# Gate and up projections of a dense FFN as three float32r products of high and low parts, with the weights split on VectorE

## The chip, the cores and the metric

The kernel runs on one core of a Trainium2 chip. The metric is the device time of one execution in microseconds, as the median of several runs. All times below are microseconds unless marked ns. The engines are TensorE (PE, its weight loads PEld), VectorE (DVE), ScalarE (ACT), GpSimd (POOL) and SyncE (SP), which issues most transfers.

## The reference, cut to what matters

Two layers run one after the other on x, 4 batches of 256 tokens with 256 features. Each layer adds a gated attention and a gated FFN: a retention-like attention and a mixture of 8 experts in layer 0, a grouped-query causal attention with 32 heads of 8 features and a dense FFN in layer 1. The change concerns the last of the four, the dense FFN, and the attention ahead of it only in time.

```python
x = x + jnp.tanh(g_xattn[1]) * _L1_xattn_ref(_layernorm(x), ctx_2048, ctx_2048, ...)
x = x + jnp.tanh(g_ffn[1]) * _L1_ffn_ref(_layernorm(x), w_gate, w_up, w_down)

def _L1_ffn_ref(x, w_gate, w_up, w_down):          # x (4,256,256), w_gate, w_up (256,1024), w_down (1024,256)
    h = jax.nn.silu(jnp.einsum('bsh,hi->bsi', x, w_gate)) * jnp.einsum('bsh,hi->bsi', x, w_up)
    h_sparse = _sparsify_2to4(h)                    # of each 4 neighbours keep the 2 largest in magnitude
    return jnp.einsum('bsi,ih->bsh', h_sparse, w_down)
```

## The kernel before, in words

It is written instruction by instruction: every engine has its own program, in the order of the code, and waits on named semaphores. Tokens are 8 tiles of 128; two halves ("units") of 512 tokens make the moving operand of gate and up. Eight PSUM banks are handed out by `acquire(pe, stage, i, kind)`: a kind is a small ring of banks, and whoever takes a bank waits until the stage that held it is `_taken`. The helper `taken` marks the instruction that reads a bank last. Kind "wide" is banks 0 to 5, "turn1" is bank 6 alone, "tok1" bank 7 alone.

*The last batch of the second attention* (b = 3) is a loop over 24 steps n. In each, TensorE makes a block of scores (`weights`), ScalarE its exponential, GpSimd masks it (`affine_select`), and at odd n one of twelve steps of `finish(2, ...)` ends the batch before: four pairs of transposes in "turn1" (VectorE divides each by its sum: reciprocal and product into `att`), a turn of `att`, the output projection, then on VectorE the residual and the statistics of the next layer norm. At steps 13, 15, 17 and 19 the first four tiles of the layer norm for the FFN go through: VectorE normalizes into `xn` (`norm`), TensorE transposes it (`ln_turn(3, k)`, bank "tok1"), ScalarE copies it to `xT` and thereby frees the bank. At the end come the products with the values.

*The dense FFN* runs over 16 pieces i = 4g + j. A piece is a gate matmul pair and an up matmul pair (`half_piece`, stages "fg" and "fu", contraction over 2 x 128 features, 128 output features x 512 tokens, all f32). ScalarE takes silu of gate, VectorE multiplies by up into `hs`, ScalarE takes the magnitude (`absh`). After each group g of four pieces VectorE runs `sparsify(g, step)` in four steps that stand between the products of the next group: three compares into bf16 (`cmps`, step 0), seven small bf16 sums (`wins`, step 1), and four masking products in steps 2 and 3. The first six pieces also carry the twelve steps of `finish(3, ...)`, and at pieces 3, 4, 6 and 7 TensorE transposes the last four tiles of the layer norm, in "turn1". `down` then multiplies by the third weight, eight tiles of eight f32 matmuls each: the first four wait until the first half of `hs` is masked, the others for the second, and they use two banks in turn, so the third waits for the residual of the first. The residuals of the first four stand between the steps of the last `sparsify` on VectorE.

The gate and up weights lie in the place of the expert weights (`e_gu`), where SyncE loads them as soon as the experts are done, long ahead of the FFN.

## Time and profile before

| | us |
|---|---|
| median of 3 runs | 383.87 |
| lowest and highest run | 381.69, 384.3 |
| span of the profiled execution, first to last instruction | 380.5 |
| of this, the dense FFN from its first matmul to the end | 93.3 |
| granted TensorE clock, mean over the span | 0.946 |

The profile gives the span of the one profiled execution, not a time of its own beside the span; the runs were timed apart. Busy times of the engines overlap, so they say who may be the bound only stretch by stretch. An f32 matmul appears in the trace as two records. The start of the next record on TensorE tells its pace better than a record's own duration, since matmuls are pipelined and their ends are modelled.

### The profile page before, as it was taken

The numbers are of one execution on the slowest core, as the hardware profiler recorded it, in microseconds if no ns is written. First come the engines' busy times: TensorE is split into PE (matmuls) and PEld (weight loads), VectorE is DVE, ScalarE is ACT, GpSimd is POOL, SyncE is SP. The second block draws the span as 40 slices with busy tenths as digits, with TensorE's granted clock in tenths as the row PEclk, the third lists the DMA queues.
The fourth block names the chain that finished last, engine by engine and source line by source line (L and its number), as shares of the span: only waits on it lengthen the run. The fifth ranks groups of instructions, "written<-read, shape, count | busy, mean of one in ns | idle before, by whom it ended". The sixth has DMA issues, their size and how long they took to land.

```text
span 380.5 us, 4562 instructions
## 1 busy us (share of the span) xinstructions
PE 334.3 (88%) x1473; PEld 201.6 (53%) x1473; DVE 220.0 (58%) x513; ACT 156.8 (41%) x327; POOL 100.2 (26%) x154
## 2 busy tenths in 40 slices
PE   3999785969999816999989999998899989999997
PEld 1485574756666404564544654643544444445885
DVE  4345976502222347889956993993342449778911
ACT  2434341333333122136867665774874233333000
POOL 7203663520000176401342334333441001000000
PEclk9999998588999756799999999999999999999999
DMA  7997000153111114500000000000000000000011
GB/s 231 364 421 210 0 15 2 65 167 101 46 53 41 55 56 166 221 0 9 0 8 2 0 0 9 0 3 8 0 2 0 2 0 0 0 1 2 28 41 41
DMA packets 14023, 22.53 MB, mean 59 GB/s; under 512 B 2049, under 2 KB 11393, under 8 KB 13186
## 3 DMA queue, kind: packets, MB, share of 16 engines
q1 hardware_dynamic: 13234, 20.16, 15.3%
q0 software_dynamic: 768, 2.10, 1.7%
q8 instruction: 12, 0.20, 0.2%
q14 instruction: 9, 0.07, 0.1%
HBM read 15.96 MB, written 6.03 MB: 58 GB/s over the span
## 4 chain that ended last, share of the span: by engine, by line
PE 65%; DVE 14%; issue 6%; POOL 5%; ACT 5%; DMA 4%; SPq 1%; ACTq 0%; DVEq 0%; POOLq 0%
PE bank L241 47%; DVE mx L1216 6%; PE bank L458 5%; PE bank L426 4%; ACT region L929 3%; PE bank L429 3%; POOL x_sorted L739 2%; PE bank L257 2%; DVE stats L999 2%; PE bank L251 2%; POOL rstd L711 1%; DVE x_sb L1039 1%; PE bank L473 1%; DMA x_sb<-in_x_dram 1%; PE bank L510 1%
## 5 line engine op out<-in xcount | busy, mean ns | idle before, releaser
L929 ACT ACTIVATE region<-bank,padcol 128x512 f32<-128x512 f32 x96 | 62.4, 695 | 18.1 <-PE bank L241 17.3
L1216 DVE TENSOR_REDUCE mx<-bank 128x2 f32<-128x512 f32 (+1 forms) x96 | 61.3, 683 | 11.7 <-PE bank L429 11.4
L241 PE MATMUL bank<-xT,e_gu 128*128 128x512 f32 x128 | 57.6, 594 | 0.5 <-ACT xT L792 0.5
L775 POOL TENSOR_SCALAR_AFFINE_SELECT region<-region 128x1024 f32<-128x1024 f32 x32 | 35.0, 1094 | 81.8 <-ACT region L929 81.7
L241 PE MATMUL bank<-qst,kblk 128*128 128x512 f32 x96 | 46.1, 490 | 0.8 <-DMA qst<-nmT 0.3
L426 PE MATMUL bank<-kblk,qst 128*128 128x512 f32 x96 | 45.1, 488 | 1.7 <-ACT qst L877 0.9
L241 PEld LDWEIGHTS bank<-xT,e_gu 128*128 128x128 f32 x128 | 23.3, 190 | 25.1 <-issue 24.3
L429 PE MATMUL bank<-causb,identb 128*128 128x256 bf16 (+1 forms) x96 | 31.8, 331 | 0.0
L241 PE MATMUL bank<-e_down,region 128*128 128x256 f32 x128 | 27.8, 379 | 0.0
L707 POOL TENSOR_SCALAR veps<-mv 128x1 f32<-128x1 f32 x40 | 11.4, 284 | 62.0 <-DVE mv L1001 59.9
L241 PEld LDWEIGHTS bank<-e_down,region 128*128 128x128 f32 x128 | 24.3, 190 | 3.7 <-issue 0.5
L1039 DVE SCALAR_TENSOR_TENSOR x_sb<-bank,tg,x_sb 128x256 f32<-128x256 f32 x24 | 11.6, 483 | 24.9 <-PE bank L241 24.8
L792 ACT ACTIVATE xT<-bank 128x256 f32<-128x256 f32 x32 | 12.3, 385 | 32.0 <-PE bank L251 31.9
L711 POOL TENSOR_TENSOR rstd<-veps,power 128x1 f32<-128x1 f32 x40 | 23.8, 595 | 3.3
L251 PE MATMUL bank<-ident,xn 128*128 128x128 f32 x48 | 12.2, 350 | 13.9 <-DVE xn L1011 11.2
L458 PE MATMUL bank<-region,vaug 128*32 128x512 f32 x192 | 23.9, 600 | 0.2
L241 PEld LDWEIGHTS bank<-qst,kblk 128*128 128x128 f32 x96 | 18.6, 196 | 9.6 <-ACT region L929 7.1
L426 PEld LDWEIGHTS bank<-kblk,qst 128*128 128x128 f32 x96 | 19.2, 200 | 8.3 <-issue 4.5
L984 ACT ACTIVATE silu<-bank 128x512 f32<-128x512 f32 x16 | 9.6, 597 | 32.5 <-PE bank L241 32.5
L1188 DVE TENSOR_TENSOR sact<-bank,silu 128x176 f32<-128x176 f32 x15 | 5.1, 342 | 30.8 <-ACT silu L895 30.8
L241 PE MATMUL bank<-e_gu,sT 128*128 x60 | 21.8, 489 | 0.5 <-ACT sT L889 0.5
L241 PE MATMUL bank<-e_down,sT 128*128 (+1 forms) x60 | 19.6, 426 | 1.4 <-ACT sT L910 1.4
(158 smaller groups left out, 543.9 us busy)
## 6 DMA issues: line engine op xcount, KB each, us to landing
e_gu<-in_e_gu_dram SPq DMA_DIRECT2D x2, 1408.0 KB, 11.9
x_sorted<-zero SPq DMA_DIRECT2D x1, 1920.0 KB, 9.1
y_sorted<-region SPq DMA_DIRECT2D x15, 128.0 KB, 1.7
x_sb<-in_x_dram SPq DMA_DIRECT2D x4, 256.0 KB, 4.2
ctxT<-in_ctxT_dram SPq DMA_DIRECT2D x2, 512.0 KB, 6.1
e_down<-in_e_down_dram SPq DMA_DIRECT2D x1, 1024.0 KB, 13.7
region<-x_sorted SPq DMA_DIRECT2D x1, 1024.0 KB, 7.3
e_gu<-in_f_gate_dram SPq DMA_DIRECT2D x1, 1024.0 KB, 4.8
```

The lines of the kernel that those rows point to most:

```text
L241: return pe.matmul(dst, lhsT, rhs, start=first, stop=last)
L251: ins = pe.transpose(dst[:, tile_cols(t)], src[:, tile_cols(t)], ident[:, :])
L426: pe.matmul(dst, qst[:, s, q, hg, tile_cols(nt)], kblk[s][q][:, quads, 0:(nt + 1) * P], start=True, stop=False, skip_group_check=True)
L429: ready(pe.matmul(diagonal, identb[:, :], causb[:, 0:diagonal.shape[1], :], start=False, stop=True, skip_group_check=True), "sa")
L458: ins = pe.matmul(dst[32 * j:32 * j + 32, :], vaug[:, 2 * b + mt, 4 * q + j, :], rhs, start=(mt == 0), stop=(mt == nt), skip_group_check=True)
L707: pool.tensor_scalar(veps[:, layer, k:k + 1], mv[:, layer, k, 1:2], eps, None, ALU.add)\
L711: pool.tensor_tensor(out=rstd[:, layer, k:k + 1], in0=veps[:, layer, k:k + 1], in1=power[:, :], op=ALU.pow).then_inc(sem(f"rstd{layer}"), 1)
L775: pool.affine_select(out=block, in_=block, compare_op=ALU.is_ge, fill=0.0, base=0, pattern=[[0, 2], [0, PER_GROUP], [1, P]], channel_multi ...
L792: taken(act.activation(xT[:, :, tile_cols(tile)], src[:, 0:DIM].rearrange("p (t n) -> p t n", t=KT), ACT.Copy), f"ln{layer}")
L929: taken(act.activation(dst, src.rearrange("p (h n) -> p h n", n=SEQ - mt * P), ACT.Exp, bias=padcol[:, key:key + 1], scale=float(HD) ** -0 ...
L1039: dve.scalar_tensor_tensor(out=x_sb[:, tile, :], in0=filled(dve, stage, k)[:, 0:DIM], scalar=tg[:, g:g + 1], in1=x_sb[:, tile, :], op0=ALU ...
L1216: taken(dve.reduce_max(mx[:, b % 2, nt, quads, q, hg], src, AX), "sa")
```

## The change

Gate and up no longer multiply f32 by f32. The transposed x and both weights are kept as a float32r high part and a float32r remainder, and each product is the sum of three: high x high, low x high and high x low. The product of the two low parts is left out. A piece of gate or up is thus six float32r matmuls instead of two f32 ones.

The high part of x is what ScalarE's copy writes (`x_high`, in the place of `xT`); a new step on VectorE, `norm_low`, subtracts it from the bank (`x_low`, in the place of `qhi` and `qlo`) and is now what frees the bank. Early tiles do this one step after the transposes (n - 1 in NORM_STEPS), late ones at pieces 4, 5 and 7 (LATE_LOW). The weights are split by eight VectorE instructions, `split_weights`, at eight steps of the last attention batch (SPLIT_AT): a cast into the high part, a subtraction in place for the low part. `gate_high` takes the place of `ctxT`, the halves of `up_high` the rest of `e_gu` and `sT`; the compares (`cmps`) move from `ctxT` to `qst`. The transposes of the last tile move from behind the up matmuls of piece 7 to before them. Several semaphores are merged, so that one count stands for several start-up loads or constants.

```diff
+LATE_LOW = {4: (4,), 5: (5,), 7: (6, 7)}
+SPLIT_AT = (0, 2, 4, 5, 6, 8, 9, 10)
...
-        cmps = ctxT[:, :, :].rearrange("p t n -> p (t n)").bitcast(BF16).rearrange("p (c n) -> p c n", n=UNIT)
+        gate_low = sb_over("gate_low", [P, KT, FFN_I], F32R, "e_gu")
+        up_low = sb_over("up_low", [P, KT, FFN_I], F32R, "e_gu", 4 * KT * FFN_I)
+        gate_high = sb_over("gate_high", [P, KT, FFN_I], F32R, "ctxT")
+        up_high = (sb_over("up_high0", [P, FFN_I], F32R, "e_gu", 8 * KT * FFN_I), sb_over("up_high1", [P, FFN_I], F32R, "sT"))
+        x_high = sb_over("x_high", [P, KT, TOKENS], F32R, "xT")
+        x_low = sb_over("x_low", [P, KT, TOKENS], F32R, "qhi")
+        halves = {"fg": ([gate_high[:, t, :] for t in range(KT)], gate_low, f_gate),
+                  "fu": ([up_high[t][:, :] for t in range(KT)], up_low, f_up)}
+
+        cmps = sb_over("cmps", [P, 6, UNIT], BF16, "qst")
...
-            def half_piece(stage, w, g, j):
+            def half_piece(stage, g, j):
+
                 u, blk = divmod(g, FFN_BLOCKS)
                 us = slice(u * UNIT, (u + 1) * UNIT)
-                c = j * 2 * P + blk * P
+                c = slice(j * 2 * P + blk * P, j * 2 * P + blk * P + P)
+                high, low, _ = halves[stage]
                 dst = acquire(pe, stage, 4 * g + j, "wide")
                 for t in range(KT):
-                    ins = mm(dst, w[:, t, c:c + P], xT[:, t, us], t == 0, t == KT - 1)
+                    mm(dst, high[t][:, c], x_high[:, t, us], t == 0, False)
+                    mm(dst, high[t][:, c], x_low[:, t, us], False, False)
+                    ins = mm(dst, low[:, t, c], x_high[:, t, us], False, t == KT - 1)
                 ready(ins, stage)
...
             pe.wait_ge(sem("ln3_taken"), UNIT_TILES)
+            pe.wait_ge(sem("w_split"), 4 * KT)
             loaded(pe, "f", 3)
             for n in range(8):
-                half_piece("fg", f_gate, n // 4, n % 4)
+                half_piece("fg", n // 4, n % 4)
                 if 2 * n < 12:
                     finish(BATCH - 1, 2 * n)
-                half_piece("fu", f_up, n // 4, n % 4)
+                if n == 7:
+                    ln_turn(3, TILES - 1, "turn1")
+                half_piece("fu", n // 4, n % 4)
                 if 2 * n < 12:
                     finish(BATCH - 1, 2 * n + 1)
-                if n in LATE_NORM_STEPS:
+                if n in LATE_NORM_STEPS[:3]:
                     ln_turn(3, UNIT_TILES + LATE_NORM_STEPS.index(n), "turn1")
...
-                taken(act.activation(xT[:, :, tile_cols(tile)], src[:, 0:DIM].rearrange("p (t n) -> p t n", t=KT), ACT.Copy),
-                      f"ln{layer}")
+                if layer == 3:
+                    act.activation(x_high[:, :, tile_cols(tile)], src, ACT.Copy).then_inc(sem("x_high_made"), 1)
+                else:
+                    taken(act.activation(xT[:, :, tile_cols(tile)], src, ACT.Copy), f"ln{layer}")
...
+            def norm_low(k):
+
+                src = filled(dve, "ln3", k)[:, 0:DIM].rearrange("p (t n) -> p t n", t=KT)
+                dve.wait_ge(sem("x_high_made"), k + 1)
+                taken(dve.tensor_tensor(out=x_low[:, :, tile_cols(k)], in0=src, in1=x_high[:, :, tile_cols(k)].bitcast(F32),
+                                        op=ALU.subtract), "ln3")
+
+            def split_weights(i):
+
+                stage, t = (("fg", 0), ("fg", 1), ("fu", 0), ("fu", 1))[i // 2]
+                high, low, raw = halves[stage]
+                if i == 0:
+                    loaded(dve, "f", 3)
+                if i % 2 == 0:
+                    dve.tensor_copy(high[t], raw[:, t, :]).then_inc(sem("w_split"), 1)
+                else:
+                    dve.wait_ge(sem("w_split"), i)
+                    dve.tensor_tensor(out=low[:, t, :], in0=raw[:, t, :], in1=high[t].bitcast(F32), op=ALU.subtract)\
+                       .then_inc(sem("w_split"), 1)
...
+                    if b == BATCH - 1 and n - 1 in NORM_STEPS:
+                        norm_low(NORM_STEPS.index(n - 1))
                     if b == BATCH - 1 and n + 2 in NORM_STEPS:
                         norm(3, NORM_STEPS.index(n + 2))
+                    if b == BATCH - 1 and n in SPLIT_AT:
+                        split_weights(SPLIT_AT.index(n))
...
+                    for k in LATE_LOW.get(i, ()):
+                        norm_low(k)
                     if 2 * i < 12:
                         finish(BATCH - 1, 2 * i)
                     src = filled(dve, "fu", i)
```

The order of instructions at three places follows. In brackets stands what an instruction waits for.

On VectorE, early in the last attention batch (`rden` and `att` are the division of `finish(2, ...)`, `x_sb` its residual), before:

```order
L1001 BN_AGGR mv<-stats 128x2 [waits stats]
L1249 RECIPROCAL rden<-bank 128x8 [waits avT_ready,atT_ready]
L1251 TENSOR_TENSOR att<-bank,rden 128x8x8 [waits rden_made]
L1249 RECIPROCAL rden<-bank 128x8 [waits avT_ready]
L1251 TENSOR_TENSOR att<-bank,rden 128x8x8 [waits rden_made]
...
L1039 SCALAR_TENSOR_TENSOR x_sb<-bank,tg,x_sb 128x256 [waits res2_ready,bias_added]
```

and after, the first of the four pairs of divisions and the stretch ahead of the residual:

```order
L1270 CAST gate_high<-e_gu 128x1024 [waits in_f]
L1293 RECIPROCAL rden<-bank 128x8 [waits avT_ready,atT_ready]
L1295 TENSOR_TENSOR att<-bank,rden 128x8x8 [waits rden_made]
L1273 TENSOR_TENSOR gate_low<-e_gu,gate_high 128x1024 [waits w_split]
...
L1295 TENSOR_TENSOR att<-bank,rden 128x8x8 [waits rden_made]
L1273 TENSOR_TENSOR up_low<-e_gu,up_high_52 128x1024 [waits w_split]
L1270 CAST up_high_53<-e_gu 128x1024
L1273 TENSOR_TENSOR up_low<-e_gu,up_high_53 128x1024 [waits w_split]
L1064 SCALAR_TENSOR_TENSOR x_sb<-bank,tg,x_sb 128x256 [waits res2_ready,bias_added]
```

Eight instructions now stand between the divisions and ahead of the residual.

On VectorE, at the change from the first group of four pieces to the second (`region` is `hs`), before:

```order
L1357 TENSOR_TENSOR region<-bank,silu 128x512 [waits fg_taken,fu_ready]
L1249 RECIPROCAL rden<-bank 128x8 [waits avT_ready]
L1251 TENSOR_TENSOR att<-bank,rden 128x8x8 [waits rden_made]
L1316 TENSOR_TENSOR ctxT<-region 128x1536 [waits abs_made]
L1318 TENSOR_TENSOR ctxT<-region 128x1024
L1320 TENSOR_TENSOR ctxT<-region 128x512
L1357 TENSOR_TENSOR region<-bank,silu 128x512 [waits fg_taken,fu_ready]
```

and after:

```order
L1407 TENSOR_TENSOR region<-bank,silu 128x512 [waits fg_taken,fu_ready]
L1293 RECIPROCAL rden<-bank 128x8 [waits avT_ready]
L1295 TENSOR_TENSOR att<-bank,rden 128x8x8 [waits rden_made]
L1364 TENSOR_TENSOR cmps<-region 128x1536 [waits abs_made]
L1366 TENSOR_TENSOR cmps<-region 128x1024
L1368 TENSOR_TENSOR cmps<-region 128x512
L1260 TENSOR_TENSOR x_low<-bank,x_high 128x2x128 [waits x_high_made,ln3_ready]
L1407 TENSOR_TENSOR region<-bank,silu 128x512 [waits fg_taken,fu_ready]
```

The subtraction for the sixth tile (`x_low`, which frees the bank "turn1") stands behind the three compares.

On TensorE, around piece 5, before (`xn` is the sixth tile of the layer norm, `att` the turn of `finish(3, 10)`):

```order
L251 MATMUL bank<-ident,xn 128x128
L241 MATMUL bank<-xT,e_gu 128x512 [waits fg_taken]
L241 MATMUL bank<-xT,e_gu 128x512
L257 MATMUL bank<-ident,att 128x128 [waits ln3_taken,avT_taken]
L257 MATMUL bank<-ident,att 128x128
L241 MATMUL bank<-xT,e_gu 128x512 [waits fu_taken]
```

and after:

```order
L269 MATMUL bank<-ident,xn 128x128
L259 MATMUL bank<-x_high,gate_high 128x512 [waits fg_taken]
L259 MATMUL bank<-x_low,gate_high 128x512
L259 MATMUL bank<-x_high,gate_low 128x512
...
L275 MATMUL bank<-ident,att 128x128 [waits ln3_taken,avT_taken]
L275 MATMUL bank<-ident,att 128x128
L259 MATMUL bank<-x_high,up_high_52 128x512 [waits fu_taken]
```

The transposes wait for the same count `ln3_taken` as before; what raises it has moved from ScalarE's copy to VectorE's subtraction.

## Rows read from the trace of the kernel before

**Rows 1.** Busy time by stretch: us, PE, PEld, DVE, ACT, POOL, PEclk, DMA share, GB/s.

```profile
287.20:322.50 35.30, 32.95 (x104) 16.14 (x100) 19.16 (x47) 11.89 (x23) 2.04 (x4) 1.00 0.00 0
322.50:350.10 27.60, 27.59 (x65) 12.29 (x66) 21.53 (x36) 9.39 (x17) 0.00 (x0) 1.00 0.00 1
```

**Rows 2.** Timeline of PE in the FFN: start, duration, engine, instruction, idle before.

```profile
287.17 1.98 PE L241 MATMUL bank<-xT,e_gu 128*128 128x512 f32 x4
...
309.77 0.44 PE L251 MATMUL bank<-ident,xn 128*128 128x128 f32 x2 [0.94 <-DVE att L1251]
...
325.61 24.63 PE L241 MATMUL bank<-xT,e_gu 128*128 128x512 f32 x57
350.08 27.79 PE L241 MATMUL bank<-e_down,region 128*128 128x256 f32 x128
```

**Rows 3.** Timeline of PE: float32r matmuls of the attention, at full clock.

```profile
198.70 0.29 PE L241 MATMUL bank<-qhi,selr 128*128 128x256 f32 x1
198.82 0.28 PE L241 MATMUL bank<-qlo,selr 128*128 128x256 f32 x1
...
205.09 0.40 PE L426 MATMUL bank<-kblk,qst 128*128 128x512 f32 x1
205.33 0.28 PE L429 MATMUL bank<-causb,identb 128*128 128x256 bf16 x1
```

**Rows 4.** Timeline of ACT behind the second late transposes.

```profile
310.24 0.38 ACT L792 ACTIVATE xT<-bank 128x256 f32<-128x256 f32 x1 [2.93 <-PE bank L251]
310.52 0.62 ACT L978 ACTIVATE region<-region 128x512 f32<-128x512 f32 x1
```

**Rows 5.** Timeline of DVE in the FFN.

```profile
315.19 0.47 DVE L1039 SCALAR_TENSOR_TENSOR x_sb<-bank,tg,x_sb 128x256 f32<-128x256 f32 x1
...
316.57 0.68 DVE L1325 TENSOR_TENSOR amat<-ctxT 128x1024 bf16<-128x1024 bf16 x1
...
326.24 0.69 DVE L1357 TENSOR_TENSOR region<-bank,silu 128x512 f32<-128x512 f32 x1 [2.50 <-PE bank L241]
326.85 1.75 DVE L1316 TENSOR_TENSOR ctxT<-region 128x1536 bf16<-128x1536 f32 x1
...
330.25 0.68 DVE L1357 TENSOR_TENSOR region<-bank,silu 128x512 f32<-128x512 f32 x1
...
333.59 0.68 DVE L1357 TENSOR_TENSOR region<-bank,silu 128x512 f32<-128x512 f32 x1
334.19 1.28 DVE L1346 SCALAR_TENSOR_TENSOR region<-amat,region 128x512 f32<-128x512 bf16 x2
```

**Rows 6.** Timeline of DVE in the last attention batch.

```profile
266.07 0.21 DVE L1249 RECIPROCAL rden<-bank 128x8 f32<-128x8 f32 x1 [2.71 <-PE bank L473]
...
273.16 0.48 DVE L1039 SCALAR_TENSOR_TENSOR x_sb<-bank,tg,x_sb 128x256 f32<-128x256 f32 x1 [3.25 <-PE bank L241]
...
276.31 0.41 DVE L1011 TENSOR_SCALAR xn<-x_sb,mv,rstd 128x256 f32<-128x256 f32 x1
...
277.39 0.69 DVE L1011 TENSOR_SCALAR xn<-x_sb,mv,rstd 128x256 f32<-128x256 f32 x1
```

**Rows 7.** Timeline of POOL in the last attention batch: causal masks.

```profile
268.13 1.10 POOL L775 TENSOR_SCALAR_AFFINE_SELECT region<-region 128x1024 f32<-128x1024 f32 x1 [3.33 <-ACT region L929]
...
276.84 1.09 POOL L775 TENSOR_SCALAR_AFFINE_SELECT region<-region 128x1024 f32<-128x1024 f32 x1 [2.73 <-ACT region L929]
```

**Rows 8.** Groups of DVE by shape, whole span: busy us, mean ns.

```profile
L1034 DVE TENSOR_SCALAR amat<-amat 128x256 f32<-128x256 f32 x2 | 0.6, 294 | 0.1
L1318 DVE TENSOR_TENSOR ctxT<-region 128x1024 bf16<-128x1024 f32 x4 | 4.9, 1220 | 0.0
```

**Rows 9.** Busy time by stretch, as rows 1: an idle stretch and two of low clock.

```profile
80.50:83.50 3.00, 0.00 (x1) 0.01 (x1) 0.04 (x1) 0.34 (x2) 0.00 (x0) 1.00 0.44 129
84.80:88.10 3.30, 3.30 (x7) 2.01 (x8) 0.28 (x1) 1.78 (x3) 0.00 (x0) 0.50 0.99 325
149.50:156.20 6.70, 5.97 (x19) 3.85 (x19) 5.08 (x12) 1.68 (x4) 5.41 (x11) 0.50 0.96 406
```

More of the change, by code:

```diff
@@ L51, in build_program, with sb_over @@
     with ctx:
+        homes = {}
         def sb(name, shape, dt=F32):
+            homes[name] = (nc.sbuf_base + 31) // 32 * 32
             return ctx.enter_context(nc.sbuf_tensor(name, shape, dt))
+        def sb_over(name, shape, dt, home, skip=0):
+            return nc.alloc_sbuf_tensor_at(name, shape, dt, offset=homes[home] + skip)
         sems = {}
@@ L329, in _ @@
             gate(1)
-            loaded(pe, "wo0")
-            loaded(pe, "router")
+            loaded(pe, "wo0", 2)
             for k in range(TILES + 4):
@@ L344, in _ @@
                     logits(k - 4)
-            pe.wait_ge(sem("onehot_made"), 1)
-            loaded(pe, "tri")
+            pe.wait_ge(sem("routed"), 1)
+            loaded(pe, "caus", 3)
             dst = acquire(pe, "rank", 0, "main")[:, 0:(TILES + 1) * EXPERTS].rearrange("p (k e) -> p k e", e=EXPERTS)
@@ L406, in keys @@
                     pe.wait_ge(sem("sel_made"), 2)
-                    pe.wait_ge(sem("padrow_made"), 1)
+                    pe.wait_ge(sem("pads_made"), 1)
                 pe.wait_ge(sem("kp_taken"), b + 1)
@@ L641, in _ @@
             load(sp, "gates", gates[:, 2:4], a["g_f"])
-            load(sp, "decay", decay[:, :, :], a["decay"])
+            load(sp, "gates", decay[:, :, :], a["decay"])
             load(sp, "wg", wg[:, :, :], a["wg"])
@@ L646, in _ @@
             load(sp, "wo0", wo0[:, :, :], a["wo0"])
-            load(sp, "router", router[:, :, :], a["router"])
-            load(sp, "small", small_c[:, :], a["small"])
+            load(sp, "wo0", router[:, :, :], a["router"])
+            load(sp, "sel", small_c[:, :], a["small"])
             load(sp, "sel", sel_in, a["sel"])
@@ L653, in _ @@
             load(sp, "sel", mask_col[:, :], a["mask_col"])
-            load(sp, "tri", tri[:, :, :], a["tri"])
-            sp.wait_ge(sem("zero_set"), 1)
+            load(sp, "caus", tri[:, :, :], a["tri"])
+            sp.wait_ge(sem("constants_set"), 1)
             sp.dma_start(x_sorted.rearrange("(s p) n -> p s n", p=P),
@@ L696, in _ @@
         def _(pool):
-            pool.memset(zero[:, :], 0.0).then_inc(sem("zero_set"), 1)
-            pool.memset(power[:, :], -0.5).then_inc(sem("power_set"), 1)
-            pool.memset(vaug[:, :, :, :], 1.0).then_inc(sem("ones_set"), 1)
-            pool.memset(amat[:, :, :], 1.0).then_inc(sem("a_set"), 1)
-            pool.wait_ge(sem("power_set"), 1)
+            pool.memset(zero[:, :], 0.0).then_inc(sem("constants_set"), 1)
+            pool.memset(power[:, :], -0.5).then_inc(sem("constants_set"), 1)
+            pool.memset(vaug[:, :, :, :], 1.0).then_inc(sem("constants_set"), 1)
+            pool.memset(amat[:, :, :], 1.0).then_inc(sem("constants_set"), 1)
+            pool.wait_ge(sem("constants_set"), 2)
             chain = [0]
@@ L734, in _ @@
             pool.wait_ge(sem("blocks_clear"), HALVES)
-            pool.wait_ge(sem("placed"), 1)
+            pool.wait_ge(sem("routed"), 3)
             pool.wait_ge(sem("sorted_zeroed"), 16)
@@ L829, in _ @@
                     ln_turn(1, k - 3)
-            act.wait_ge(sem("vdiff"), 1)
+            act.wait_ge(sem("routed"), 2)
             act.activation(r_s[:, 3, :], r_s[:, 2, :], ACT.Exp).then_inc(sem("vexp"), 1)
@@ L840, in projections @@
                 if b == 0:
-                    act.wait_ge(sem("ones_set"), 1)
+                    act.wait_ge(sem("constants_set"), 3)
                 for t in range(2):
@@ L895, in slot_silu @@
                 act.activation(silu[:, i % 2, 0:EXPERT_I], src, ACT.Silu).then_inc(sem("silu_made"), 1)
-            act.wait_ge(sem("padrow_made"), 1)
+            act.wait_ge(sem("pads_made"), 1)
             slot_turn(0)
@@ L922, in exponentials @@
                 if n == 0 and b == 0:
-                    act.wait_ge(sem("padcol_made"), 1)
+                    act.wait_ge(sem("pads_made"), 2)
                     act.wait_ge(sem("x2"), TILES)
@@ L1020, in _ @@
                     norm(0, k - 2)
-            loaded(dve, "decay")
-            dve.wait_ge(sem("a_set"), 1)
+            loaded(dve, "gates", 3)
+            dve.wait_ge(sem("constants_set"), 4)
             for h in range(RET_HEADS):
@@ L1041, in residual @@
                    .then_inc(sem(stage + "_taken"), 1)
-            loaded(dve, "sel", 3)
-            loaded(dve, "small")
+            loaded(dve, "sel", 4)
             dve.tensor_scalar(padrow[:, :], mask_row, 0.0, MASKED, ALU.is_equal, ALU.mult)\
-               .then_inc(sem("padrow_made"), 1)
+               .then_inc(sem("pads_made"), 1)
             dve.tensor_scalar(padcol[:, :], mask_col[:, :], 0.0, DEAD, ALU.is_equal, ALU.mult)\
-               .then_inc(sem("padcol_made"), 1)
+               .then_inc(sem("pads_made"), 1)
             def gn_center(k):
```

24 lines of the change are left out of this document (12 added, 12 removed).

## The prediction

> **What bounds the kernel now.** I read the last 93 us of the span, because the change leaves everything up to the fourth batch of the second attention as it was. First the table of busy time by stretch [rows 1]: while gate and up run, TensorE is busy 32.95 of 35.30 us and then 27.59 of 27.60, and VectorE 19.16 and 21.53. So TensorE is the bound there, but VectorE has only about 6 us in hand in the second stretch. Then TensorE's timeline [rows 2]: the dense FFN begins at 287.17, the first of 32 pieces of gate or up (two f32 matmuls, four records) takes some 1.8 us, and late in the stretch 57 records take 24.47 us, 0.43 us each or 1.72 us a piece. The down projection then runs 128 records of 0.217 us without a gap and ends the kernel. The granted clock is 1.00 throughout. VectorE's steady round for four pieces is in [rows 5]: product 0.61, compares 3.40 (326.85 to 330.25), product 0.61, counts 2.73, then twice a product and a pair of masking products, 0.60 and 1.28. That is 11.1 us, against 8 x 1.72 = 13.8 us of TensorE.
>
> **TensorE's pieces.** A piece becomes six float32r matmuls of 512 columns. The nearest rows [rows 3]: two float32r matmuls of 256 columns, each with its own stationary load, start 0.12 us apart; one of 512 columns is followed after 0.24 us. Between twice 0.1067 (256 columns at 2.4 GHz) plus 0.003 (the overhead of a 0.43 us f32 record) and 0.24 I take 0.225, nearest to the first row's overhead of 0.011: 1.35 us a piece, bounds 1.30 and 1.44. All 32 pieces then save 32 x 0.37 = 11.8 us of TensorE. The Trainium skill, "TensorE: Matmul & The Clock Gate", section "Back-to-back issue gap", gives columns over 2.4 GHz plus about 2.5 ns; an estimate from it is 0.216 us, and the sum below would be better by 0.7 us. The row of 0.12 us at full clock shows more overhead than that.
>
> **VectorE's subtractions hold a bank.** This is where most of the saving goes. Before, ScalarE's copy released the bank of each normalized tile; now VectorE's subtraction x_low releases it, and the four late ones use the one bank that TensorE's attention transposes need as well. The order of VectorE puts x_low of the sixth tile behind the 3.40 us of compares, and TensorE's next transposes wait for it. Before, from 287.17 to the second late transposes at 309.77 [rows 2] is 22.60 us: ten pieces (17.2) and 5.4 of transposes and waits, which stay. With 1.35 a piece they come 18.9 us after the start. ScalarE copies the tile and then takes the magnitudes that the compares need: these end 1.37 after the transposes [rows 4]; compares 3.40, and x_low with its hand-over 0.48 (as the residual at 315.19 [rows 5], the same 256 columns). So TensorE goes on 5.29 us after the transposes; with 0.27 for them and 1.35 for one piece it **stands 3.67 us**.
>
> Then it needs 0.22 for the waiting transposes, 1.35 for a piece, and 1.13 for the attention's last projection (four records of 0.217) and the hand-over; VectorE spends 1.40 on residual, statistics and normalization (315.19 to 316.57 and a hand-over [rows 5]), 2.73 on counts, 0.60 and 0.32 on product and normalization, 1.28 on masking, and 0.48 on x_low of the seventh tile. Only then may the last tile be transposed, 33.7 us after the start, while TensorE has finished everything ahead of that after 30.95: it **stands 2.76 us** more. Three pieces and 0.47 of transposes and hand-over later the ninth product runs, at 38.2 us. Before it ran at 326.24, 39.07 after the start. **In the first half the FFN gains 0.8 us**, not 6.
>
> From the ninth product on TensorE (8 x 1.35 = 10.8 a round) is ahead of VectorE (11.1), and VectorE's rounds set the time: 11.1 to the thirteenth product, then 9.2 to the sixteenth, 20.3; before, the sixteenth ran 0.2 after 350.08, 24.0 later: **3.7 gained**. At the end the down projection's third tile waits for the first one's residual, which now comes behind the last product, masking, compares and residual: 5.86; six tiles of 16 x 0.217 follow, 20.7, so 26.6 from the sixteenth product to the end, and before 27.4: **0.8 gained**. In all 5.3 us, with VectorE as the bound and not TensorE.
>
> **The split in the last attention phase.** Eight instructions of 1,024 columns. A subtraction is priced by the f32 compare of that size, 1.22 busy [rows 8] and, as products of 0.69 follow one another after 0.61 [rows 5], about 1.14 to the next start; a cast has no row: at one column a cycle 1.22, at the rate of the f32 operation with one input in [rows 8] (256 columns in 0.294 where a residual takes 0.48) about 0.69 and 0.60 to the next. I take the latter, the row nearest in kind. VectorE is idle 2.71 us before 266.07 [rows 6], so the first cast is free; the other seven and the three pairs between them fill it from 266.07 to 273.9, and the residual that stood at 273.16 comes 0.75 later. On it hang the normalization, the transposes and, in turn, all that follows. GpSimd's causal masks of 1.1 us run in the same stretch [rows 7], and where one runs, a VectorE operation with one input waits: the normalization at 277.39 took 0.69 instead of the usual 0.41, ending when the mask that began at 276.84 was over. I count one such wait, 0.5. The four early x_low release their bank 0.45 after the copy did, and this shifts the start of the last values once: 0.45. Sum 1.7 us; bounds 0.5 (the queue of exponentials absorbs the rest) and 3.9 (casts at one column a cycle, +1.6, and one more half mask, +0.6). Loads of the weights are long done, ScalarE's eight copies cost what they did, cmps only moves, and the merged semaphores of the start wait for loads that were waited for anyway: nothing.
>
> **The clock.** After the idle stretch 80.5 to 83.5 the granted clock fell to 0.50 (1.2 GHz) some 1.3 us after work had begun again, for 3.3 us; another low stretch lasted 6.7 us [rows 9]. The waits of 0.94 us at 309.77 left it at full. Both new stands are well over the latter, so I expect a fall after each, as in the first of these rows. After the first, 1.3 us cover the waiting piece and the projection behind it takes 0.86 more; the next two pieces are not waited for. After the second, two pieces that are waited for run in the low stretch: half of 3.3, 1.65. Together 2.5; bounds 0 and, low from the start and for 6.7 us, 2.2 + 3.35 = 5.5.
>
> **Sum.** 5.3 gained less 1.7 less 2.5 is 1.1 us of the profiled span of 380.5, so 379.4. The span lies 3.4 under the median of the runs, 383.87, and 1.2 under the fastest; I carry the difference over: **382.7 us**, 0.3% faster. About 1% is what a measurement of this kernel can tell from no change.
>
> **The rivals.** (1) *The clock holds* through both stands, as it did through the waits of 0.94: 383.87 - 3.6 = 380.2; with 1.30 a piece and a split that costs 0.7 it is 378.5. Against it: no idle stretch of the length predicted is in the rows without a fall. (2) *VectorE and GpSimd block each other*: four masks, the first at 268.13, fall within 6 us beside seven split instructions. If each holds VectorE for its whole 1.1 us, that is 4.4 instead of the 0.5 counted, 3.9 more, and the time is 386.6, slower than before. It turns to slower once more than 1.1 us is added. For it speaks the 0.69 at 277.39; against it, that a cast begun first would make the mask wait instead, and that masks have slack. The Trainium skill, "SBUF — State Buffer", section "Who interferes with whom", says that an operation with two inputs in SBUF also contends with a GpSimd operation that reads SBUF, which would take in the four subtractions; no row here shows that. (3) *The bank does not hold TensorE*, the compares being early enough: 11.8 - 1.7 gives 373.8. The order of both engines and the measured 1.37 speak against it. (4) *The change doesn't do what it says*: float32r at 512 columns at the 0.43 of an f32 record, so three products cost 192 x 0.43 = 82.6 us, +27.5: 411. The 0.24 in [rows 3] excludes nearly all of it.
>
> **How the numbers follow.** Forecast 0.46, clock holds 0.24, blocking 0.20, no hold 0.08, slow float32r 0.02. Half of the second case and all of the fourth lie below 380.0, with a tail of the forecast (casts cheap, one fall only): faster by over 1% 0.23. Above 387.7 lie a third of the blocking case, the last case and the forecast's worst bounds (low clock for 6.7 us twice with the dear split: 5.3 - 3.9 - 5.5 = -4.1): slower 0.12. Within 1% 0.65. The range 379.0 to 387.0 takes in the first three cases but their tails.
>
> **What would show it.** Right: two waits of TensorE on x_low, of about 3.7 and 2.8 us, some 20 and 31 us after the FFN's first matmul, a granted clock of 0.50 after each; VectorE busy without idle from the ninth product to the last masking; pieces of 1.35 us; the FFN's start 1 to 2 us later than 287.17. Wrong: no such waits, or a clock of 1.00 behind them; casts of 1.2 us; split instructions much longer than those of a quiet GpSimd; TensorE gap-free from gate to down.

## The result and the profile after

The changed kernel takes 386.99 us, the median of four runs (386.18 to 387.81), and the kernel before 384.09 beside it (four runs, 381.69 to 384.45; 383.87 was the median of the first three): a ratio of 1.009, 95% interval 1.0059 to 1.0121. It is 0.9% slower, where 0.3% faster was forecast. The profiled execution is the slowest of its four runs, as that of before is the fastest of its own; it spans 385.8 us, 5.3 more than before. Of this 1.2 lie ahead of the change: the fifth tile's residual ran at 262.20 before and at 263.38 now. In four more profiled executions with the changed code up to there it ran at 262.06 and 262.12 (*filler_att* and *low_first* below) and at 263.50 and 263.51 (*filler* and *masks_cut*), so this much differs between executions of the same code; why is open. All distances below are therefore taken from that residual.

VectorE's timeline of the changed kernel in the last attention phase answers to [rows 6]: start, duration, engine, line and instruction.

```profile
263.38 0.48 DVE L1064 SCALAR_TENSOR_TENSOR x_sb<-bank,tg,x_sb 128x256 f32<-128x256 f32 x1 [1.69 <-PE bank L259]
...
264.45 0.66 DVE L1270 CAST gate_high<-e_gu 128x1024 fp32r<-128x1024 f32 x1
...
267.62 1.21 DVE L1273 TENSOR_TENSOR gate_low<-e_gu,gate_high 128x1024 fp32r<-128x1024 f32 x1
...
269.13 0.68 DVE L1270 CAST gate_high<-e_gu 128x1024 fp32r<-128x1024 f32 x1
...
270.13 1.72 DVE L1273 TENSOR_TENSOR gate_low<-e_gu,gate_high 128x1024 fp32r<-128x1024 f32 x1
271.78 1.58 DVE L1270 CAST up_high<-e_gu 128x1024 fp32r<-128x1024 f32 x1
...
273.65 1.74 DVE L1273 TENSOR_TENSOR up_low<-e_gu,up_high 128x1024 fp32r<-128x1024 f32 x1
...
276.02 2.07 DVE L1273 TENSOR_TENSOR up_low<-e_gu,up_high 128x1024 fp32r<-128x1024 f32 x1
278.02 0.47 DVE L1064 SCALAR_TENSOR_TENSOR x_sb<-bank,tg,x_sb 128x256 f32<-128x256 f32 x1
```

GpSimd's masks in the same stretch answer to [rows 7]:

```profile
269.30 1.47 POOL L798 TENSOR_SCALAR_AFFINE_SELECT region<-region 128x1024 f32<-128x1024 f32 x1 [2.91 <-ACT region L954]
271.61 2.70 POOL L798 TENSOR_SCALAR_AFFINE_SELECT region<-region 128x1024 f32<-128x1024 f32 x2 [0.84 <-ACT region L954]
275.93 1.09 POOL L798 TENSOR_SCALAR_AFFINE_SELECT region<-region 128x1024 f32<-128x1024 f32 x1 [1.62 <-ACT region L954]
```

Read the two side by side. A cast alone takes 0.66 and a subtraction alone 1.21. Where the two engines overlap, the one that began second is longer: three subtractions took 1.72 to 2.07, a cast 1.58, and of the masks one took 1.47 and two 2.70 together, instead of 1.09 each. The cast at 269.13 and the mask at 275.93 began first and kept 0.68 and 1.09. Each of the three subtractions ended 1.07 or 1.08 us after the mask that it had met, so nearly all of its work came behind the mask. An x_low, which reads one of its two operands from PSUM, lay wholly beside a mask and kept its 0.42:

```profile
282.09 1.26 POOL L798 TENSOR_SCALAR_AFFINE_SELECT region<-region 128x1024 f32<-128x1024 f32 x1 [5.07 <-ACT region L954]
```

```profile
282.52 0.42 DVE L1260 TENSOR_TENSOR x_low<-bank,x_high 128x256 fp32r<-128x256 f32 x1
```

TensorE's timeline, as [rows 2], with the idle time before a row in brackets:

```profile
273.87 0.41 PE L275 MATMUL bank<-ident,att 128*128 128x128 f32 x2 [2.35 <-DVE att L1295]
...
279.63 0.66 PE L269 MATMUL bank<-ident,xn 128*128 128x128 f32 x2 [2.99 <-DVE xn L1036]
...
293.21 0.50 PE L259 MATMUL bank<-x_high,gate_high 128*128 128x512 f32 x1
293.55 0.39 PE L259 MATMUL bank<-x_low,gate_high 128*128 128x512 f32 x1
293.78 0.39 PE L259 MATMUL bank<-x_high,gate_low 128*128 128x512 f32 x1
...
317.95 0.66 PE L275 MATMUL bank<-ident,att 128*128 128x128 f32 x2 [3.55 <-DVE x_low L1260]
...
318.83 0.63 PE L259 MATMUL bank<-x_low,up_high 128*128 128x512 f32 x1
319.26 0.63 PE L259 MATMUL bank<-x_high,up_low 128*128 128x512 f32 x1
...
329.71 0.44 PE L269 MATMUL bank<-ident,xn 128*128 128x128 f32 x2 [1.92 <-DVE x_low L1260]
```

The two stands on x_low are there, 3.55 and 1.92 us long. Before them are two that nobody forecast, in the attention, where transposes wait for what VectorE does behind the split. The matmuls follow one another after 0.23 us at full clock and 0.43 after the first x_low stand. What the clock did is in the table of busy time by stretch, of PE, PEld, DVE, ACT and POOL; the number ahead of the last two is the granted clock, 1.00 for 2.4 GHz and 0.50 for 1.2 GHz, averaged over the stretch:

```profile
279.00:283.00 4.00, 3.37 (x12) 2.55 (x12) 2.75 (x10) 2.57 (x5) 0.91 (x1) 0.57 0.00 0
283.00:293.00 10.00, 9.48 (x68) 3.62 (x66) 4.41 (x12) 5.84 (x12) 5.16 (x8) 1.00 0.01 2
293.00:317.00 24.00, 19.52 (x96) 15.06 (x92) 11.71 (x30) 8.59 (x15) 0.88 (x3) 1.00 0.00 1
317.00:324.00 7.00, 6.05 (x16) 4.87 (x17) 2.44 (x6) 0.90 (x2) 0.00 (x0) 0.51 0.00 0
324.00:330.00 6.00, 4.08 (x21) 3.02 (x20) 5.62 (x14) 2.10 (x4) 1.17 (x2) 1.00 0.00 0
330.00:334.00 4.00, 4.00 (x13) 3.21 (x12) 2.24 (x4) 0.90 (x2) 0.00 (x0) 0.58 0.01 2
334.00:356.00 22.00, 22.00 (x96) 17.77 (x95) 19.95 (x34) 9.27 (x16) 0.00 (x0) 1.00 0.00 1
```

Three falls to 1.2 GHz, of which one lies in the attention; before, [rows 1] shows 1.00 through all of gate and up. The ends of the stretches that the prediction counted in are these rows of VectorE: the ninth product, the sixteenth, and the last residual.

```profile
335.92 0.69 DVE L1407 TENSOR_TENSOR region<-bank,silu 128x512 f32<-128x512 f32 x1 [1.84 <-PE bank L259]
...
356.24 0.69 DVE L1407 TENSOR_TENSOR region<-bank,silu 128x512 f32<-128x512 f32 x1
...
383.20 0.48 DVE L1064 SCALAR_TENSOR_TENSOR x_sb<-bank,tg,x_sb 128x256 f32<-128x256 f32 x1 [2.97 <-PE bank L259]
```

Before, the ninth product stood at 326.24 [rows 5]. The fifth tile's residual, the sixteenth product and the last residual stood here:

```profile
262.20 0.48 DVE L1039 SCALAR_TENSOR_TENSOR x_sb<-bank,tg,x_sb 128x256 f32<-128x256 f32 x1 [1.68 <-PE bank L241]
...
350.28 0.69 DVE L1357 TENSOR_TENSOR region<-bank,silu 128x512 f32<-128x512 f32 x1 [1.07 <-PE bank L241]
...
377.90 0.48 DVE L1039 SCALAR_TENSOR_TENSOR x_sb<-bank,tg,x_sb 128x256 f32<-128x256 f32 x1 [2.97 <-PE bank L241]
```

So from the residual to the FFN's first matmul 29.83 us (before 24.97), to the ninth product 42.71 (39.07), to the sixteenth 20.32 (24.04) and to the last residual 26.96 (27.62). The second half and the end gained 4.4, where 4.5 was forecast. The two stretches ahead of them lost 8.5, where 1.7 and 1.7 were forecast.

### The profile page after: what moved, and what is told of

The parts are those of the page before. It is cut to its first block, busy times and chain, and to the rows that moved or that the text cites. A ratio compares the mean times of both kernels' runs of the same rounds, so it can differ in the third digit from the quotient of the medians.

```text
span 385.8 us, 4706 instructions
## 1 busy us (share of the span) xinstructions
PE 330.4 (86%) x1530; PEld 218.0 (57%) x1537; DVE 232.5 (60%) x529; ACT 157.8 (41%) x327; POOL 101.8 (26%) x154
## 4 chain that ended last, share of the span: by engine, by line
PE 62%; DVE 18%; issue 6%; POOL 5%; DMA 4%; ACT 3%; SPq 1%; another core or an unknown queue 0%; DVEq 0%; ACTq 0%; POOLq 0%
PE bank L259 44%; DVE mx L1240 6%; PE bank L474 5%; PE bank L442 4%; PE bank L445 2%; POOL x_sorted L762 2%; PE bank L269 2%; PE bank L275 2%; DVE stats L1024 2%; POOL rstd L734 1%; PE bank L489 1%; DVE x_sb L1064 1%; DMA x_sb<-in_x_dram 1%; ACT region L954 1%; PE bank L526 1%
## 5 line engine op out<-in xcount | busy, mean ns | idle before, releaser
L798 POOL TENSOR_SCALAR_AFFINE_SELECT region<-region 128x1024 f32<-128x1024 f32 x32 | 36.1, 1128 | 85.2 <-ACT region L954 85.2
L445 PE MATMUL bank<-causb,identb 128*128 128x256 bf16 (+1 forms) x89 | 28.6, 321 | 0.0
L730 POOL TENSOR_SCALAR veps<-mv 128x1 f32<-128x1 f32 x40 | 10.8, 271 | 63.8 <-DVE mv L1026 61.7
L734 POOL TENSOR_TENSOR rstd<-veps,power 128x1 f32<-128x1 f32 x40 | 24.9, 623 | 3.3
L259 PEld LDWEIGHTS bank<-qst,kblk 128*128 128x128 f32 x96 | 18.9, 203 | 8.4 <-ACT region L954 6.1
L442 PEld LDWEIGHTS bank<-kblk,qst 128*128 128x128 f32 x96 | 18.9, 197 | 8.3 <-issue 4.4
L445 PEld LDWEIGHTS bank<-causb,identb 128*128 128x128 bf16 x96 | 9.4, 98 | 20.3 <-issue 17.2
L269 PEld LDWEIGHTS bank<-ident,xn 128*128 128x128 f32 x48 | 6.1, 172 | 24.4 <-issue 13.2
L818 ACT ACTIVATE xT<-bank 128x256 f32<-128x256 f32 x24 | 9.2, 381 | 22.8 <-PE bank L269 22.6
```

The costliest lines, as they stand in the source:

```text
L259: return pe.matmul(dst, lhsT, rhs, start=first, stop=last)
L269: ins = pe.transpose(dst[:, tile_cols(t)], src[:, tile_cols(t)], ident[:, :])
L442: pe.matmul(dst, qst[:, s, q, hg, tile_cols(nt)], kblk[s][q][:, quads, 0:(nt + 1) * P], start=True, stop=False, skip_group_check=True)
L445: ready(pe.matmul(diagonal, identb[:, :], causb[:, 0:diagonal.shape[1], :], start=False, stop=True, skip_group_check=True), "sa")
L730: pool.tensor_scalar(veps[:, layer, k:k + 1], mv[:, layer, k, 1:2], eps, None, ALU.add)\
L734: pool.tensor_tensor(out=rstd[:, layer, k:k + 1], in0=veps[:, layer, k:k + 1], in1=power[:, :], op=ALU.pow).then_inc(sem(f"rstd{layer}"), 1)
```

## The experiments

Theory A: VectorE's split and GpSimd's masks block each other on the path to the FFN. Theory B: x_low, behind the compares, keeps a bank that TensorE needs. Theory C: the stands cost a second time, through the clock. The rivals are that the split costs its own duration and no more (D), and that VectorE, not the stands, sets the first half. All ten kernels in one table, by the same four stretches of their profiled executions (us):

| kernel | to FFN | to 9th product | to 16th | to end | ratio to before, 95% interval |
|---|---|---|---|---|---|
| before | 24.97 | 39.07 | 24.04 | 27.62 | 1 |
| changed | 29.83 | 42.71 | 20.32 | 26.96 | 1.009 (1.0059 to 1.0121) |
| masks_cut | 26.22 | 40.51 | 20.32 | 26.96 | 0.9975 (0.9954 to 0.9997) |
| before_masks_cut | 24.69 | 39.08 | 24.03 | 27.63 | 0.9989 (0.9969 to 1.0009) |
| split_spread | 25.50 | 40.73 | 20.27 | 26.96 | 0.9938 (0.9915 to 0.9961) |
| low_first | 30.33 | 35.21 | 20.32 | 26.96 | 0.9903 (0.9879 to 0.9927) |
| filler | 29.21 | 39.13 | 20.27 | 26.96 | 1.0007 (0.9989 to 1.0026) |
| filler_att | 29.20 | 41.94 | 20.32 | 26.96 | 1.0075 (1.0046 to 1.0105) |
| both | 25.52 | 36.53 | 20.33 | 26.96 | 0.980 (0.9774 to 0.9826) |
| both_filler | 25.51 | 35.19 | 20.27 | 26.96 | 0.9806 (0.9786 to 0.9825) |

### masks_cut: the split without masks beside it

```diff
+                        r = (2, PER_GROUP) if b < BATCH - 1 else (1, 1)
+                        block = block[:, 0:r[0], 0:r[1], :]
                         pool.affine_select(out=block, in_=block, compare_op=ALU.is_ge, fill=0.0, base=0,
-                                           pattern=[[0, 2], [0, PER_GROUP], [1, P]], channel_multiplier=-1)\
+                                           pattern=[[0, r[0]], [0, r[1]], [1, P]], channel_multiplier=-1)\
```

> The changed kernel with GpSimd's eight causal masks of the fourth batch cut from 128x1024 to 128x128 each, so that they hold nothing for 1.1 us; what lies right of the diagonal in the other blocks is not set to zero. Theory A (a mask and a VectorE operation on SBUF hold each other up): the four split instructions that took 1.58 to 2.07 us fall to 0.68 (cast) and 1.21 (subtraction), together 2.8 us less; the residual at 278.02 comes some 2.5 us sooner, the wait of 2.99 us on the normalization shrinks to about 0.5 and the clock stays at 1.00 there; the time falls by 2.5 to 4 us, to 383 to 384.5. Rival D (the eight split instructions cost this much by themselves, whatever GpSimd does): the four keep their 1.6 to 2.1 us, the residual stays within 0.5 us, the time within 1 us of 387.

Measured: 382.18 us, ratio 0.9975, by the ratios 4.4 us less than the changed kernel, where 2.5 to 4 were expected. VectorE's split and the residual behind it, and GpSimd's cut masks:

```profile
270.27 1.22 DVE L1275 TENSOR_TENSOR gate_low<-e_gu,gate_high 128x1024 fp32r<-128x1024 f32 x1
271.40 0.69 DVE L1272 CAST up_high<-e_gu 128x1024 fp32r<-128x1024 f32 x1
...
272.38 1.22 DVE L1275 TENSOR_TENSOR up_low<-e_gu,up_high 128x1024 fp32r<-128x1024 f32 x1
...
274.32 1.23 DVE L1275 TENSOR_TENSOR up_low<-e_gu,up_high 128x1024 fp32r<-128x1024 f32 x1
275.47 0.48 DVE L1066 SCALAR_TENSOR_TENSOR x_sb<-bank,tg,x_sb 128x256 f32<-128x256 f32 x1
```

```profile
272.90 0.84 POOL L800 TENSOR_SCALAR_AFFINE_SELECT region<-region 128x128 f32<-128x128 f32 x1 [0.67 <-ACT region L956]
274.66 1.04 POOL L800 TENSOR_SCALAR_AFFINE_SELECT region<-region 128x128 f32<-128x128 f32 x1 [0.92 <-ACT region L956]
279.14 0.29 POOL L800 TENSOR_SCALAR_AFFINE_SELECT region<-region 128x128 f32<-128x128 f32 x1 [3.44 <-ACT region L956]
```

The subtractions are back at 1.22, and the residual stands 11.96 us behind the earlier one, instead of 14.64 in the changed kernel and 10.96 before: 2.68 us were blocking and 1.00 the split's own. D falls. The block goes both ways: a mask of 0.29 took 1.04 beside a subtraction. The stands in the attention shrank to 0.95 and 1.73 (about 0.5 was expected of the second), and the clock held there. In the FFN's first half one fall came instead of two, which makes it 2.2 us shorter.

### before_masks_cut: the control

The same edit in the kernel before.

> The control for the run with the masks cut: the kernel before, with the eight causal masks of the fourth batch cut from 128x1024 to 128x128 (the other blocks keep what lies right of the diagonal). Theory A: without a split nothing but one normalization (0.69 instead of 0.41) met a mask, and the last masks stand ahead of the last values for about 1 us, so the FFN's first matmul comes 0 to 1.5 us sooner after the residual of the fifth tile than the 24.97 us of before, ratio 0.995 to 1.00. Rival: the masks themselves are on the path all along, and cutting them gains as much here as it did in the changed kernel, 3 us or more, ratio 0.99 or less; then the 2.7 us of blocking were no cost of the change.

Measured: 382.58 us, ratio 0.9989; the FFN begins 0.28 us sooner. Without the split the masks cost 0.3 us in the profiled execution, and in the runs nothing clear of the noise. What *masks_cut* gained beyond that is what the split and the masks did to each other, and the falls of the clock that came of it.

### split_spread: the split where VectorE waits

```diff
-SPLIT_AT = (0, 2, 4, 5, 6, 8, 9, 10)
+SPLIT_AT = {(0, 23): (0,), (1, -1): (1,), (1, 21): (2,), (1, 22): (3,), (1, 23): (4,), (2, -1): (5,), (2, 23): (6, 7)}
...
-                    if b == BATCH - 1 and n in SPLIT_AT:
-                        split_weights(SPLIT_AT.index(n))
...
+                    for i in SPLIT_AT.get((b, n), ()):
+                        split_weights(i)
```

The keys are batch and step (-1: between the row maxima that lead the batch), the values say which of the eight.

> The changed kernel with the eight split instructions moved out of the last attention phase: they stand one or two at a time at the ends and beginnings of the first three batches, where VectorE waits 1.3 to 2.9 us for TensorE in the trace of before. Theory A (the last phase has no room for the split beside the masks): the last phase goes as before but for x_low, the FFN's first matmul comes 3 to 5 us sooner than 293.2, the clock does not fall in the attention, the time falls by 3 to 5 us, to 382 to 384. Rival D' (the split costs its own duration wherever it stands, since VectorE is on the path all through the attention): 7.2 us of work stay on the path, the FFN's start and the time within 1 us.

Measured: 381.03 us, ratio 0.9938. Seven of the eight took 0.66 to 0.69 and 1.22 to 1.23; one cast took 1.08, beside GpSimd's bias. The second residual stands 10.95 us behind the first, as before, and the FFN begins 25.50 after it: 0.53 more than before, which is all that the four early x_low cost. D' falls. The last two of the eight run in the wait ahead of 266.07 [rows 6], the other six ahead of the fifth tile's residual; that these cost nothing there follows from the times: the four stretches together are 2.2 us shorter than before, and by the ratio the whole kernel is 2.4. The clock held in the attention. The first half still has both stands, and one fall:

```profile
313.73 0.46 PE L275 MATMUL bank<-ident,att 128*128 128x128 f32 x2 [3.56 <-DVE x_low L1260]
...
324.82 0.44 PE L269 MATMUL bank<-ident,xn 128*128 128x128 f32 x2 [2.43 <-DVE x_low L1260]
```

### low_first: x_low ahead of the compares

```diff
-LATE_LOW = {4: (4,), 5: (5,), 7: (6, 7)}
+LATE_LOW, LOW_FIRST = {4: (4,), 7: (7,)}, {4: 5, 6: 6}
...
+                    if i in LOW_FIRST:
+                        norm_low(LOW_FIRST[i])
                     if g >= 1:
                         sparsify(g - 1, j)
```

> The changed kernel with two of VectorE's x_low moved: that of the sixth tile ahead of the 3.40 us of compares, that of the seventh ahead of a pair of masking products. No work is added or left out. Theory B (the bank that x_low holds makes TensorE stand): the stand of 3.55 us falls under 0.5, that of 1.92 under 1.0; the clock does not fall after the first; the ninth product comes 4 to 6 us sooner after the FFN's first matmul than the 42.7 us of the changed kernel, and the time falls by 3 to 6 us, to 381 to 384. Rival (VectorE sets the first half anyway, so its order does not matter): the ninth product stays within 1 us and so does the time.

Measured: 379.53 us, ratio 0.9903. VectorE and, below it, TensorE at that place:

```profile
312.76 0.42 DVE L1260 TENSOR_TENSOR x_low<-bank,x_high 128x256 fp32r<-128x256 f32 x1 [1.02 <-ACT x_high L816]
313.21 1.76 DVE L1364 TENSOR_TENSOR cmps<-region 128x1536 bf16<-128x1536 f32 x1
...
322.27 0.42 DVE L1260 TENSOR_TENSOR x_low<-bank,x_high 128x256 fp32r<-128x256 f32 x1
```

```profile
313.47 0.38 PE L275 MATMUL bank<-ident,att 128*128 128x128 f32 x2
...
322.75 0.44 PE L269 MATMUL bank<-ident,xn 128*128 128x128 f32 x2 [2.10 <-DVE x_low L1260]
```

The first stand is gone and the ninth product comes 7.5 us sooner after the FFN's start, more than the 4 to 6 expected: no fall followed in the FFN at all, which by *filler* below is 3.6 of it. In the attention, left as in the changed kernel, this execution had a longer fall, and the FFN began 0.5 us later. The second stand stayed, against the expectation: the seventh tile's x_low went ahead of the masking, but it still stands behind the counts and a product. VectorE lost nothing by the order: it waited 1.02 us for the copy, where it waited 1.47 for the magnitudes in the changed kernel, and the compares begin 20.76 us after the FFN's start in both.

### filler: TensorE kept busy in the stands

```diff
+            def fill(kind, count):
+                bank = KINDS[kind][turns[kind] % len(KINDS[kind])]
+                before, m = occupant[bank]
+                pe.wait_ge(sem(before + "_taken"), m + 1)
+                for _ in range(count):
+                    mm(banks[bank][:, :], selr[:, 0:P], kblk[1][0][:, 0:2, :].rearrange("p j n -> p (j n)"), True, True)
...
+                    if b == BATCH - 1 and n in (9, 13):
+                        fill("max", 9 if n == 9 else 12)
...
+                if n == 5:
+                    fill("wide", 14)
...
                 if n == 7:
+                    fill("wide", 10)
                     ln_turn(3, TILES - 1, "turn1")
```

The results go into the bank that the next piece fills anyway.

> The changed kernel with float32r matmuls of 512 columns, whose results are overwritten, put where TensorE stands: 9 and 12 in the last attention phase, 14 ahead of the wait of 3.55 us and 10 ahead of that of 1.92; they leave all waits as they are. Theory C (the stands cost twice, since the granted clock falls after them): the clock is 1.00 from the last attention phase to the end; of the 5.7 and 2.4 us of work at half speed in the FFN some 4 us are saved, less what goes into a longer second wait: the time falls by 1.5 to 4 us. Rival (VectorE and not TensorE's pace sets the time between the two stands): the clock stays at 1.00 and the time within 1 us of 387. If the clock falls all the same, C stays untested.

Measured: 383.67 us, ratio 1.0007, some 3.2 us less than the changed kernel by the ratios. The waits on VectorE stay, filled with work, and the clock is 1.00 throughout (busy time by stretch):

```profile
263.00:293.00 30.00, 27.91 (x156) 14.41 (x155) 20.27 (x43) 18.29 (x35) 14.21 (x17) 1.00 0.01 3
293.00:332.00 39.00, 36.73 (x170) 28.69 (x170) 22.27 (x53) 13.46 (x25) 2.05 (x4) 1.00 0.00 1
```

The first half went from 42.71 to 39.13, and the attention from 29.83 to 29.21: 3.58 and 0.62 are what the clock cost in the changed kernel's profile. That is 1.0 more than the 3.2 by the ratios; the profile was taken of the changed kernel's slowest run. C holds, and its rival falls.

### filler_att: busy in the attention alone

The same edit without its two places in the FFN.

> The changed kernel with the matmuls that are overwritten in the last attention phase alone (9 and 12), none in the FFN. With all of them the clock stayed at 1.00 throughout. Theory C1 (each stand brings its own fall): the clock holds in the attention, and falls after the stand of 3.55 us and again after the second of about 2; the first half takes 42 to 43 us, 1 us less than the changed kernel in all. Theory C2 (what went before counts: with no fall in the attention the FFN has one fall only, as in the runs with the masks cut and the split spread): first half 40.5 to 40.8 us, the time 2.5 us less than the changed kernel, ratio about 1.002.

Measured: 385.58 us, ratio 1.0075; first half 41.94 with two falls, as C1 has it. But in *masks_cut* and *split_spread*, which also had no fall in the attention, the second stand of 2.4 us was followed by none. Neither C1 nor C2 covers all three.

### both: the two moves together

The edits of *split_spread* and *low_first*.

> The two moves together: the split spread over the first three batches, and two x_low ahead of the compares and the masking. From the runs so far: FFN start 25.5 us after the residual of the fifth tile (as with the split spread), ninth product 35.2 us after the start (as with x_low first), 20.3 to the sixteenth, 27.0 to the end. If the two costs are separate (theories A and B), this is 5.5 us less than with the split spread alone: about 375.5 us, ratio to before 0.98. Rival: the two overlap (one stand pays for both), and the time stays within 1.5 us of the better of the two, 379.5.

Measured: 375.68 us (374.28 to 377.82), ratio 0.980, interval 0.9774 to 0.9826: 2.0% faster than before, as separate costs were to give; the rival falls. The gains by the ratios do not quite add up: over the changed kernel the two moves gain 1.5% and 1.9% alone and 2.9% together, since each alone already spares part of the falls (with the split spread one is left, with x_low first none in the FFN). TensorE's one stand that is left, and the clock behind it:

```profile
319.74 0.44 PE L269 MATMUL bank<-ident,xn 128*128 128x128 f32 x2 [2.09 <-DVE x_low L1260]
```

```profile
263.00:321.00 58.00, 50.96 (x267) 32.51 (x266) 32.22 (x85) 30.75 (x58) 16.09 (x21) 1.00 0.01 2
321.00:325.00 4.00, 4.00 (x12) 2.94 (x11) 2.32 (x4) 0.60 (x2) 0.00 (x0) 0.57 0.01 2
```

### both_filler: the last stand filled

The edits of *both*, and `fill("wide", 8)` ahead of the last tile's transposes.

> The two moves together, and eight float32r matmuls of 512 columns, whose results are overwritten, ahead of the one stand that is left (2.09 us before the last tile's transposes). Of the runs so far such a stand of 1.9 to 2.4 us was followed by a fall in three profiled executions and not in three. Theory C (a fall after this stand costs 1.3 us, and it comes in most executions): the clock stays at 1.00, the ninth product comes 35.2 us after the FFN's first matmul instead of 36.5, the median falls by 0.7 to 1.3 us, ratio 0.9765 to 0.978. Rival: falls after it are the exception, or VectorE takes over the same 1.3 us: ratio 0.980 as without.

Measured: 375.85 us, ratio 0.9806, no different from *both*. In the profiled execution the clock is 1.00 and the ninth product comes at 35.19, as C expected; in the median nothing is gained. The profiled execution of *both* was its slowest run (377.82), but whether the fall came in its other four is not shown: their mean clocks over the span, 0.931 to 0.940, lie on both sides of its 0.932. So it is open whether falls here are the exception or VectorE takes their cost over. Five runs show no gain from filling this stand.

## Why the prediction was wrong, point by point

**The step that failed: "The split in the last attention phase ... I count one such wait, 0.5 ... Sum 1.7 us".** The mechanism was named and its size was wrong. The FFN began 4.86 us later: 1.00 of the split's own work (0.75 forecast), **2.68 of blocking** (0.5 forecast), 0.53 of the early x_low (0.45 forecast) and 0.62 of a clock fall in the attention (none forecast). The upper bound of 3.9 did not hold it either. I had one row of blocking, a one-input operation, and let only one instruction be held up by a mask; four were, three of them subtractions with both inputs in SBUF. That they are blocked as well was in the prediction, but as a rival with a chance of 0.20. The Trainium skill, "SBUF — State Buffer", section "Who interferes with whom", says that an instruction of VectorE with two SBUF inputs contends with one of GpSimd that reads SBUF. This case's trace agrees: 1.22 alone, 1.72 to 2.07 beside a mask.

So the second rival came true in its mechanism, with 2.2 us more than was counted instead of 3.9, and in its sign; it was to turn to slower beyond 1.1. That its 386.6 lies 0.4 from the measured 386.99 is luck: the blocking was 1.7 us smaller than it says, and the clock cost 1.7 more than the forecast that it starts from. That 386.99 still lies inside the range up to 387.0 is luck too, since the sign of the sum was wrong.

**The clock: 2.5 forecast, 4.2 measured** (3.58 in the FFN and 0.62 ahead of it), the second term that was too small. Falls came where they were forecast, but the first began at 317, while TensorE still stood, and lasted 6.8 us, as the longer of the two stretches in [rows 9] did. My bound of 5.5 held. The third fall, in the attention, followed from the blocking, which had made stands of 2.35 and 2.99 there.

**The bank: right.** First stand 3.55, behind transposes that came 19.35 us after the FFN's start (18.9 forecast). The forecast of 3.67 holds a slip: 1.37, 3.40 and 0.48 make 5.25 and not 5.29, so its own terms give 3.63. The second was 1.92 (2.76), since TensorE was slower by then; in *masks_cut* and *split_spread*, with 3.4 us of low clock ahead of it, it was 2.4. The fix takes 7.5 us out of the first half, 3.6 of them the clock's.

**The pieces: right, but a little dearer than taken.** 0.232 us a matmul and 1.40 a piece, where 0.225 and 1.35 were taken. Over the ten pieces to the first stand this is the 0.45 us between 19.35 and 18.9. The whole first half takes 39.13 without a fall (*filler*), 0.9 more than the 38.2 forecast; the other half of this was not taken apart. So, as far as *filler* shows, the first half had nothing to gain, not 0.8.

**VectorE as the bound from the ninth product: right in the number, not in the reason.** 20.32 against 20.3 forecast, in every kernel with the change, 20.27 to 20.33; the end 26.96 against 26.6 (before it took 27.62, not 27.4). But TensorE was to be ahead with 10.8 us for four pieces against VectorE's 11.1, and at 1.40 a piece it needs 11.2. It is busy 22.00 of 22.00 us from 334 to 356, and the thirteenth product waits for it: VectorE ends a masking pair at 346.95, TensorE's last matmul for the product ends at 347.06, and the product begins at 347.09.

```profile
345.67 1.28 DVE L1394 SCALAR_TENSOR_TENSOR region<-amat,region 128x512 f32<-128x512 bf16 x2
347.09 0.69 DVE L1407 TENSOR_TENSOR region<-bank,silu 128x512 f32<-128x512 f32 x1
```

```profile
346.66 0.40 PE L259 MATMUL bank<-x_high,up_low 128*128 128x512 f32 x1
```

So up to there TensorE set the pace, by 0.14 us, and VectorE, which waits no more after it, set the rest. No run separates the two.

**The sum.** Forecast +5.3 -1.7 -2.5 = 1.1 gained. Measured in the same terms, -0.06 + 3.72 + 0.66 = 4.3 gained, less 4.24 for the attention without its clock, less 4.20 for the clock: 4.1 lost. The medians differ by 2.9. The profiled execution of before was its fastest (381.69, up to 384.45) and that of the changed kernel its slowest (387.81, from 386.18), so 1.2 of the 4.1 lie within what executions differ by, and the clock's share is the least certain of the terms.

**What stays open.** What decides whether a fall follows the last stand. After 1.92 (changed), 2.09 (*both*) and 2.43 (*filler_att*) it fell; after 2.10 (*low_first*), 2.43 (*split_spread*) and 2.44 (*masks_cut*) it did not. The length of the stand does not order them, nor does an earlier fall.

## What to carry to other kernels

Before putting work into an engine's idle time, look at what its neighbour does in the same microseconds: here some 7.5 us of VectorE work (four casts of 0.66, four subtractions of 1.21) cost nothing that the times show when spread over gaps in three batches, and 3.7 us in the idle time of the last, 2.7 of them because GpSimd's masks ran there. An operation that releases a PSUM bank belongs ahead of long work in its engine's order. The two moves together, the split spread and the bank released early, turned a change that lost 0.9% into one that gains 2.0%. Where a forecast hangs on a count of collisions, count each instruction that can meet one, and price the stands that follow at both clocks.

## What the runs showed of the hardware that was not expected

- A mask on GpSimd and a cast or a subtraction on VectorE with all operands in SBUF hold each other up, in both directions: 1.22 became 1.72 to 2.07, 0.66 became 1.58, and a mask of 0.29 became 1.04. An x_low, with one operand in PSUM, kept 0.42 beside a mask.
- The granted clock fell while TensorE stood, not only after it had begun again: at 317.0 in the changed kernel, 0.9 us ahead of the first matmul behind the stand. Low stretches lasted 3.4 us (*masks_cut*, *both*), 6.8 (the second of the changed kernel) and 10.2 (*low_first*, from 274.0, in the attention, between stands of 2.36 and 1.83).
- Six float32r matmuls of 512 columns that add into one bank follow one another after 0.232 us at 2.4 GHz and 0.43 at 1.2 GHz.
